# A two-layer decoder on one core: the output product of the first cross-attention in high and low parts

## The reference

```
q_hk = (hidden_q @ Wq.T).reshape(Bv, Sv, H, K)
q_big = einsum('bshk,hkq->bshq', q_hk, w_kc_q), rotated
q_r, k_r = q_big @ W_qr, rotated context @ W_kr
attn = softmax(einsum('bhsr,bhlr->bhsl', q_r, k_r))      # 256 x 1601 for each head
ctx_c = einsum('bhsl,bld->bhsd', attn, kv_r)             # 16 heads of 64 channels
ctx_lat = einsum('bhsd,hkd->bhsk', ctx_c, w_kc_kv)
return ctx_lat (heads side by side) @ Wo.T
...
dispatch = einsum('tec,th->ech', sec_mask, tokens)       # 8 experts, 160 slots each
hmid = gelu(einsum('ech,ehi->eci', dispatch, w1)); expert_out = einsum('eci,eih->ech', hmid, w2)
```

## Time and profile before

| | us |
|---|---|
| time, median of 3 runs | 1401.38 (1399.49 to 1403.59) |
| the profiled execution's own time | 1405.69 |
| span of the profiled execution | 1403.9 |
| mean granted TensorE clock | 0.946 |
| PE busy | 1280.9 |
| DVE busy | 809.9 |
| ACT busy | 615.2 |
| POOL busy | 820.2 |

### The profile page before, as it was taken

The page is one execution under the profiler, slowest core; times in us unless marked ns, Lnnn a source line. Parts: engine busy times, 40 slices in busy tenths (PEclk is TensorE's granted clock), DMA queues, the critical chain, the costliest instruction groups (busy, mean ns, idle before and its releaser), DMA issues.

```text
span 1403.9 us, 20138 instructions
## 1 busy us (share of the span) xinstructions
PE 1280.9 (91%) x7051; PEld 832.6 (59%) x7051; DVE 809.9 (58%) x1439; ACT 615.2 (44%) x1643; POOL 820.2 (58%) x747
## 2 busy tenths in 40 slices
PE   7999998999999999999979576998999999989793
PEld 4865545666666666666647563444676884547582
DVE  4756666667666666666623426766666123664443
ACT  3731113454454444444430324887666115771151
POOL 1266005999999999999980534988544003560444
PEclk9999997999999999999989687999999997998897
DMA  8501110000000000000008320000000105200263
GB/s 256 132 9 38 31 38 19 9 8 12 9 8 9 12 9 8 8 13 9 8 1 276 105 62 21 1 0 1 1 1 1 27 0 153 61 2 30 67 141 117
DMA packets 67532, 60.12 MB, mean 43 GB/s; under 512 B 19440, under 2 KB 64392, under 8 KB 66920
## 3 DMA queue, kind: packets, MB, share of 16 engines
q1 hardware_dynamic: 64408, 50.56, 12.9%
q0 software_dynamic: 3024, 8.26, 2.5%
HBM read 40.58 MB, written 9.83 MB: 36 GB/s over the span
## 4 chain that ended last, share of the span: by engine, by line
PE 77%; POOL 6%; DVE 5%; ACT 5%; issue 4%; DMA 1%; another core or an unknown queue 0%; POOLq 0%; DVEq 0%; SPq 0%; ACTq 0%
PE PS L481 71%; PE PS L489 5%; ACT s_sc L1278 2%; POOL PWS L1904 2%; POOL a_m L1964 2%; POOL a_m L1958 2%; DVE s_mx L1689 1%; ACT a_m L1235 1%; POOL slot_rows L1944 1%; DVE pm L1489 1%; DVE HN L1380 1%; PE PS L638 0%; PE PS L675 0%; POOL s_sc L1979 0%
## 5 line engine op out<-in xcount | busy, mean ns | idle before, releaser
L1904 POOL TENSOR_TENSOR PWS<-PWS 128x1024 f32<-128x1024 f32 x160 | 379.2, 2370 | 45.9 <-ACT PWS L1179 26.7
L1489 DVE TENSOR_REDUCE pm<-PS 128x2 f32<-128x1024 f32 x192 | 226.0, 1221 | 106.3 <-PE PS L481 106.1
L1179 ACT ACTIVATE PWS<-PS 128x512 f32<-128x512 f32 (+1 forms) x416 | 212.4, 600 | 79.0 <-PE PS L481 73.9
L481 PE MATMUL PS<-PWS,KVR 128*64 128x256 f32 (+1 forms) x1664 | 185.2, 379 | 0.0
L481 PE MATMUL PS<-QALL,KH 128*128 128x512 f32 (+1 forms) x416 | 181.2, 436 | 0.1
L481 PE MATMUL PS<-QM,KL 68*128 68x512 f32 (+1 forms) x416 | 165.8, 398 | 0.0
L1979 POOL TENSOR_SCALAR s_sc<-s_sc,s_ri 128x128 f32<-128x128 f32 (+1 forms) x256 | 103.9, 425 | 101.3 <-DVE s_ri L1696 101.3
L481 PEld LDWEIGHTS PS<-PWS,KVR 128*64 128x64 f32 (+1 forms) x1664 | 121.0, 137 | 58.6 <-issue 0.2
L481 PEld LDWEIGHTS PS<-QALL,KH 128*128 128x128 f32 (+1 forms) x416 | 77.1, 185 | 76.8 <-ACT PWS L1179 59.1
L1278 ACT ACTIVATE s_sc<-PS,s_nb 128x128 f32<-128x128 f32 (+1 forms) x256 | 104.3, 431 | 3.9 <-DVE s_nb L1692 3.9
L1185 ACT ACTIVATE CTX<-PS 128x256 f32<-128x256 f32 x32 | 12.3, 384 | 194.5 <-PE PS L481 194.5
(11 more groups left out here) (307 smaller groups left out, 2396.4 us busy)
## 6 DMA issues: line engine op xcount, KB each, us to landing
QALL<-qlo SPq DMA_DIRECT2D x32, 128.0 KB, 2.4
QM<-QALL SPq DMA_DIRECT2D x64, 64.0 KB, 2.0
f_w<-in_L_ffn_w_dram SPq DMA_DIRECT2D x2, 2048.0 KB
tile_results<-e_y SPq DMA_DIRECT2D x31, 128.0 KB
a_nat<-in_L_attn_w_qkv_dram SPq DMA_DIRECT2D x1, 3072.0 KB, 22.2
x_wq<-in_L_xattn_Wq_dram SPq DMA_DIRECT2D x1, 2048.0 KB, 10.6
x_wo<-in_L_xattn_Wo_dram SPq DMA_DIRECT2D x2, 1024.0 KB, 7.0
a_wo<-in_L_attn_w_o_dram SPq DMA_DIRECT2D x1, 2048.0 KB, 20.8
```

Of the source, the lines that this page charges most:

```text
L481: return nc.tensor.matmul(o, a, b, start=start, stop=stop, **kw)
L1179: nc.scalar.activation(PW[c][0:rows, j * HALF:(j + 1) * HALF], st_bank("block", LT * u + lt)[0:rows, :], ACT.Exp).then_inc(p_ready, 1)
L1489: V.tensor_reduce(pm[u % 2][:, :, i // 3, i % 3], src, AX, ALU.max).then_inc(nat_read, 1)
L1904: G.tensor_tensor(ACC[:, :], PW[0][:, :] if i == 0 else ACC[:, :], PW[i + 1][:, :], ALU.add).then_inc(acc_step, 1)
```

## The change

Stage 4 takes its product in one-pass F32R products. DVE splits the context behind each normalisation: the high part goes by a copy to a free place of QALL, the low part is subtracted in place (CTXL lies over CTX). Output weights are split the same way in units 23 to 30 (UL lies over U). PE runs 24 one-pass products for a tile instead of 8 f32 ones. Since QALL now stays in use during stage 4, the expert weights, which lie over it, are loaded later: SP issues them behind the clearing of the slot rows, on a semaphore of their own for which PE waits at the first expert. The three small loads keep their place.

```
+        CTXL = at("CTXL", 151744, [P, PAIRS, B * T], F32R)
+        UL = at("UL", 184576, [P, PAIRS, C], F32R)
+        def context_high(b, p):
+            return QALL[:, p % 4, b, p // 4, :]
+        def weights_high(p):
+            return QALL[:, 6, p // 2, p % 2, :] if p < 6 else QALL[:, 7, 0, p % 2, :]
+        SPLIT_FROM = 2 * PAIRS + 7
...                                                                       # PE, stage 4
-                out_product(("xo", t), [(CTX[:, p, t * P:(t + 1) * P], U[:, p, :]) for p in range(PAIRS)])
+                b, at_ = t // 2, t % 2 * P
+                ps = begin(("xo", t), "dve")
+                split_product(ps[:, 0:C], [(context_high(b, p)[:, at_:at_ + P], CTXL[:, p, t * P:(t + 1) * P],
+                                            weights_high(p), UL[:, p, :]) for p in range(PAIRS)]).then_inc(filled, 1)
...                                                                       # PE, stage 5; DVE waits likewise
-            pe.wait_ge(moe0_loaded, 16 * 5)
+            pe.wait_ge(moe0_loaded, 16 * 3)
...                                                                       # PE, up0(e)
+                if e == 0:
+                    pe.wait_ge(experts_loaded, 32)
...                                                                       # DVE, normalised(u)
                 V.tensor_tensor(out_, out_, sums, ALU.mult).then_inc(norm_done, 1)
+                dve.wait_ge(norm_done, u + 1)
+                V.tensor_copy(context_high(b, p), out_).then_inc(ch_ready, 1)
+                dve.wait_ge(ch_ready, u + 1)
+                V.tensor_tensor(CTXL[:, p, b * T:(b + 1) * T], out_, context_high(b, p).bitcast(F32), ALU.subtract)
+            def weights_split(p):
+                V.tensor_copy(weights_high(p), U[:, p, :]).then_inc(uh_ready, 1)
+                dve.wait_ge(uh_ready, p + 1)
+                V.tensor_tensor(UL[:, p, :], U[:, p, :], weights_high(p).bitcast(F32), ALU.subtract)
...                                                                       # DVE, end of unit u
+                if SPLIT_FROM <= u < SPLIT_FROM + PAIRS:
+                    weights_split(u - SPLIT_FROM)
...                                                                       # SP
-            sp.dma_start(f_w1[:, :, :, :], L0_ffn_w1.rearrange("e (k p) i -> p e k i", p=P)).then_inc(moe0_loaded, 16)
-            sp.dma_start(f_w2[:, :, :, :], L0_ffn_w2.rearrange("e (k p) i -> p e k i", p=P)).then_inc(moe0_loaded, 16)
...                                                                       # SP, behind the store of cleared slot rows
+            sp.dma_start(f_w1[:, :, :, :], L0_ffn_w1.rearrange("e (k p) i -> p e k i", p=P)).then_inc(experts_loaded, 16)
+            sp.dma_start(f_w2[:, :, :, :], L0_ffn_w2.rearrange("e (k p) i -> p e k i", p=P)).then_inc(experts_loaded, 16)
```

## The result

| | before | after |
|---|---|---|
| median, us | 1400.47 (4 runs, 1399.49 to 1403.59) | 1422.49 (4 runs, 1415.51 to 1423.59) |
| ratio, 95% interval | 1 | 1.0140 [1.0113, 1.0167] |
| profiled execution, its span | 1405.69, 1403.9 | 1423.59, 1421.8 |

The change makes the kernel 22.0 us slower; the forecast was 1410, 8.6 over the 1401.38 that it started from. A second group of runs of the two kernels gave 1409.97 against 1392.18, ratio 1.0135 [1.0106, 1.0164].

A forecast was written before the change was run, and what follows sets the result against it. PE was taken to bound the kernel, with POOL nearly as long in the attention stage. -4.2 + 2.0 + 9.0 + 0.75 + 0.75 = +8.3 us on the 1401.38 median gave 1409.7, stated as 1410, range 1395 to 1417.

The forecast's parts named there:

- The product, -4.2: Output product: 192 one-pass products at 0.122 us plus 2.27 for the half clock, 4.2 us less than before.
- Rival (b): Output product at 0.109 us each and no effective DVE-POOL collision in the attention stage: 1395.5 us; chance 0.15.
- rival (c): Output product: weight loads not hidden under short streams, up to 43.8 us, 1418 with no hold; chance 0.05.
- The context pairs, +2.0: Attention stage: held context copy and subtraction make PE 0.3 us late in 12 units without keys to turn; 2.0 taken.
- The hold: Attention stage: new DVE copies and subtractions wait for a running POOL addition to end, at most 2.37 us before each.
- Rival (a): Attention stage: DVE and POOL don't collide to effect, the subtraction slips in behind the copy; 1398 to 1399, chance 0.30.
- The alternation, every second weights pair: Units 23 to 30: a stalled unit puts POOL ahead, so the next pair is free; 4 of 8 units stall.
- 3 x 3.0 = 9.0: Output-weights pairs in the attention stage: three stalls count, each a PE wait of 3.0 us, adding 9.0 us.
- The last lies under POOL's final 6 us: End of the attention stage: the fourth weights-pair stall is hidden while PE waits 6 us for POOL; cost 0.
- The end, +0.75 and +0.75: Attention stage's end: holds by three pairs in POOL's last two units, 0.75 us; last copy and subtraction in the open, 0.75.
- The loads, 0: Expert weights: the later loads arrive about 15 us before their first reader, so they cost 0.
- Rival (d): Units 23 to 30: every weights pair stalls, 7 x 3.0 us, or expert weights come too late; 1422, chance 0.06.

The follow-up runs named there:

- both_psum: Changed kernel with new DVE operations kept off SBUF-to-SBUF by way of PSUM, weights pairs moved behind the all-maxima reduction; ratio to before 0.9972, repeated 0.9987.
- contexts_only: Changed kernel without the eight output-weights pairs (not computed), the 32 context pairs kept; 1401.74 us, ratio to before 1.0011.
- weights_only: Changed kernel without the 32 context pairs (not computed), the eight weights pairs kept in place; ratio to before 0.9938.
- filled: Changed kernel with 27 unused one-pass products added ahead of the seven later blocks in units 24, 26, 28 and 30; ratio to before 1.0203.
- load_only: Kernel before with only the expert-weight loads moved behind the clearing of the slot rows; ratio to before 0.9986.
- sub_held: Changed kernel without weights pairs; the context copy reads PSUM, the context subtraction has both inputs in SBUF; ratio to before 0.9936.
- weights_late: Changed kernel with the eight weights pairs moved to the end, behind the last context pair; 1400.65 us, ratio to before 0.9998.
- weights_moved: Changed kernel with the weights pairs, still from SBUF, moved behind the all-maxima reduction; ratio to before 1.0081.

## Why the prediction was wrong

- **The product, -4.2: right, in part by luck.** -4.25. The residual additions 772.97 and 775.80 stand 2.83 apart, 0.118 for each of 24 products; I had taken 0.122.

```profile
767.13 0.42 DVE L1421 TENSOR_TENSOR X<-X,PS 128x256 f32<-128x256 f32 x1 [5.68 <-PE PS L496]
...
772.97 0.42 DVE L1421 TENSOR_TENSOR X<-X,PS 128x256 f32<-128x256 f32 x1 [1.94 <-PE PS L496]
775.80 0.42 DVE L1421 TENSOR_TENSOR X<-X,PS 128x256 f32<-128x256 f32 x1 [1.95 <-PE PS L496]
```

  The first came 5.60 after the product's start, 2.77 over the spacing (2.27 forecast). So the spacing was 0.8 us too dear in all and the half clock 0.5 too cheap, and the two nearly cancel; in both_psum, where the clock rose sooner, the same products save 5.6. Rival (b), 0.109, would have needed 2.62 and rival (c) 5.5 apart.
- **The context pairs, +2.0: right in size, not in place.** POOL stands at 611.02 instead of 608.69, +2.33, of which 0.5 had come before the stage; contexts_only and before differ by 1.6 between units 7 and 23. I had 0.3 in each of 12 units without keys to turn. By POOL's starts, units 9 and 17 give 0.5 each, the other units without keys under 0.1, and those with keys up to 0.12. That the sum fits is luck.
- **The hold: right, both kinds.** Rival (a) falls: the subtraction did not slip in behind the copy (608.09, 1.45 long). It does so where POOL idles (632.35 above, 615.02 in weights_only).
- **The alternation, every second weights pair: right. Its price, 3 x 3.0 = 9.0: wrong, and this is the failed step.** Measured 22.2. Two things are in it. I let PE wait at its second late plain score, which needs the middle reductions. But the tail's PSUM bank is one of the three through which the score blocks rotate, so PE stops at the third block of BACK, about 2.5 us sooner: 3.06 us of idle time. That wait is by chance as long as the 3.0 I had. What I left out altogether is what follows an idle stretch: the granted clock fell to 0.50, its half level (1.2 GHz), for 6 us, 3.0 us of PE time more. So three stalls cost 6.3 each and not 3.0, and a fourth, which I had at 0, cost 3.6. I had the same effect at the head of the product in the earlier trace rows and in my own sum (the 2.27) and did not carry it over to a new wait. filled shows it to be the cause: with PE kept busy in that gap the clock stayed at 1.00 and the unit was 2.9 shorter.
- **"The last lies under POOL's final 6 us": wrong.** The stall of unit 30 cost 18.91 - 15.32 = 3.6. It is paid in PE's stream, which feeds the exponentials that POOL adds, so POOL's chain begins later by it.
- **The end, +0.75 and +0.75: the open last pair right, the holds too high.** The copy at 760.70 and the subtraction at 761.03 hold the product back by 0.78; of the 1.1 in contexts_only 0.3 are left for the holds in POOL's last units.
- **The loads, 0: right** (load_only).

Put together with the measured terms: -4.25 + 1.8 + 22.2 + 1.1 = +20.9; the medians differ by 22.0, the second group by 17.8. Rival (d) gave 1422 and met the time, but not for its reason: only every second pair stalls, at 6.3 us, not each at 3.0.

What stays open: some ratios differ from what their traces give up to the product's end: weights_only and sub_held are 0.3 and 0.4% below, weights_late 0.2% below, weights_moved 0.3% above. The unchanged work behind the product varies by more than that with the granted clock; why it does so in a given run was not looked into.

## What to carry to other kernels

Before putting DVE work beside a busy GpSimd, look where its operands lie: one more copy through PSUM cost 0.42 us here, and operations that had lasted 1.0 to 1.7 us in the mean took 0.42. Price a new PE wait as the wait and what the clock may cost behind it (here 3.06 became 6.3), and find it by the first buffer that the late operation frees, not by the last. A stall that makes the next unit free of stalls hides half the damage; moving or shortening it can bring that half back.

## What was not expected of the hardware

- Short idle times of PE were followed by a lower clock: 0.50 and 0.63 us of wait within 2.5 us by 5.5 us at 0.69, 2.14 us by 5 us at 0.66, 3.06 us by 6 us at 0.50. A single wait of 0.66 us in weights_only was not.
- A copy from SBUF to SBUF, f32 to F32R, 128x256, is 0.29 us when nothing holds it; the same from PSUM 0.42. So the short form is the one that is held (the longest record of L1547 in the changed kernel is 2.30 us).
- A copy from SBUF into PSUM was never held (417 ns, eight of eight, among POOL's additions).
